# Row stages in chunks of 128 rows in place of 256, beside an LSTM that runs step by step

## What is computed

```
att = agg.reshape(n, 512) @ Wo.T + bo          # agg: attention sums, divided by their denominators
x2  = xn + att
z   = layernorm(x2) * g + b
h   = silu(z @ W1.T + b1)                      # 512 -> 1024
x   = x + x2 + h @ W2.T + b2                   # 1024 -> 512
y   = layernorm(x)
# LSTM over the rows as time, t = 0..1249, hidden size 512, four gates
gates_t = y_t @ Wx + b + h_{t-1} @ Wh
c_t = sigmoid(f) * c_{t-1} + sigmoid(i) * tanh(c~);  h_t = sigmoid(o) * tanh(c_t)
x   = x + h_t
```

## Time and profile before

| | us |
|---|---|
| median of 3 runs | 6714.76 |
| lowest, highest | 6714.20, 6720.42 |
| span of the profiled execution | 6560.1 |
| median of the runs less that span | 154.7 |
| PE busy | 5245.2 (80% of the span) |
| DVE busy | 3804.3 (58%) |
| ACT busy | 1879.1 (29%) |

### The profile page before, as it was taken

How to read it: one execution, slowest core, us unless ns; L and a number is a source line. 1 busy time by engine, 2 the same in 40 slices (tenths; PEclk the granted TensorE clock), 3 DMA queues, 4 the chain that set the end, 5 groups by cost and what they waited for, 6 DMA issues and landing times. The chain is left out here.

```text
span 6560.1 us, 407056 instructions
## 1 busy us (share of the span) xinstructions
PE 5245.2 (80%) x179105; PEld 3616.3 (55%) x179105; DVE 3804.3 (58%) x22336; ACT 1879.1 (29%) x8915; POOL 677.8 (10%) x716
## 2 busy tenths in 40 slices
PE   1989757789777888777887778987777777888999
PEld 1433334566555666556665556665555555554445
DVE  7337857466666666666666666666666666574111
ACT  1210069333333333333333333333333333200100
POOL 0744345000000000000000000000000000252000
PEclk8999979899999999999999999999999999998999
DMA  2235455101000000000000000100000000221110
GB/s 90 77 92 141 117 160 162 59 28 30 1 0 0 17 28 17 0 0 8 27 27 0 0 0 22 30 9 0 0 0 0 0 0 0 77 80 56 68 36 13
DMA packets 172012, 241.50 MB, mean 37 GB/s; under 512 B 90362, under 2 KB 130938, under 8 KB 167827
## 3 DMA queue, kind: packets, MB, share of 16 engines
q0 software_dynamic: 41952, 116.33, 6.5%
q1 hardware_dynamic: 129714, 120.73, 6.0%
HBM read 224.38 MB, written 12.61 MB: 36 GB/s over the span
## 5 line engine op out<-in xcount | busy, mean ns | idle before, releaser
L1654 PE MATMUL l_bank<-l_w,l_hp 128*32 128x128 f16 x160000 | 2486.7, 220 | 823.4 <-DVE l_hp L1942 801.0
L1654 PEld LDWEIGHTS l_bank<-l_w,l_hp 128*32 128x32 f16 x160000 | 2255.6, 97 | 1431.7 <-DVE l_hp L1942 1391.2
L1906 DVE STREAM_TRANSPOSE agg<-l_bank 128x128 f32<-128x128 f32 x2500 | 792.9, 317 | 1176.6 <-PE l_bank L1654 1005.9
L1782 ACT ACTIVATE l_th<-l_z 128x8 f32<-128x8 f32 x2500 | 523.7, 209 | 2153.2 <-DVE l_z L1912 2153.2
L1664 PE MATMUL l_spare<-l_w 128*2 128x512 f16 x12120 | 865.0, 379 | 3.7 <-issue 3.7
L2128 POOL DMA_INDIRECT ga_rows<-r_table,dst_t x176 | 166.9, 948 | 4633.8 <-DMA r_table<-c_r 4508.2
L1787 ACT ACTIVATE l_tc<-l_th 128x2 f32<-128x2 f32 x2500 | 490.5, 196 | 465.5 <-DVE l_th L1929 465.5
L1918 DVE SCALAR_TENSOR_TENSOR l_terms<-l_th 128x4 f32<-128x4 f32 x2500 | 357.0, 143 | 256.7 <-ACT l_th L1782 256.7
L1936 DVE TENSOR_TENSOR l_hp<-l_go,l_tc 128x2 f16<-128x2 f32 x2500 | 422.0, 169 | 132.0 <-ACT l_tc L1787 0.9
L1912 DVE TENSOR_REDUCE l_z<-agg 128x8 f32<-128x24 f32 x2500 | 447.5, 179 | 42.6
L1942 DVE TENSOR_TENSOR l_hp<-l_full,l_hp 128x2 f16<-128x2 f32 x2500 | 422.6, 169 | 43.9 <-DVE l_full L1937 0.6
(11 more groups left out here) (428 smaller groups left out, 4913.8 us busy)
## 6 DMA issues: line engine op xcount, KB each, us to landing
w<-in_g_W SPq DMA_DIRECT2D x128, 128.0 KB, 2.1
w<-in_l_Wx SPq DMA_DIRECT2D x128, 128.0 KB, 2.1
keys<-in_src_by_tile SPq DMA_DIRECT2D x7, 1344.0 KB, 6.8
e_w<-in_e_W SPq DMA_DIRECT2D x2, 4096.0 KB
e_chosen<-chosen SPq DMA_DIRECT2D x24, 256.0 KB, 6.2
wh<-in_l_Wh SPq DMA_DIRECT2D x1, 4096.0 KB, 18.8
late<-in_l_Wh SPq DMA_DIRECT2D x1, 4096.0 KB, 19.0
late<-in_l_Wx SPq DMA_DIRECT2D x1, 4096.0 KB
```

The source lines that it names most:

```text
L1654: mm = pe.matmul(banks[par][q][32 * j:32 * j + 32, 0:128], hp[:, par, k, 30 - 30 * v:62 - 30 * v], w16[:, half, k, j, 256 * q + 128 * v:25 ...
L1782: act.activation(th[:, 2 * q:2 * q + 2, 1:], z[:, q, :].rearrange("p (j m) -> p j m", m=GATES), ACT.Tanh, scale=2.0 ** -Z_BITS).then_inc(s ...
L1906: dve.transpose(turn[:, par, q, :, 1:33], banks[par][q][:, 0:128].rearrange("p (m r) -> p m r", r=32)).then_inc(s_turned[q], 1)
```

## The change

W becomes 128, so there are ten chunks: one before the recurrence and nine beside it, of 128 steps each, 102 of them with row work; steps 1152 to 1249 have none. A row operation has 128 columns in place of 256, and a turn one transpose in place of two.

The first chunk's Wx no longer goes into `late` behind the packing. Its first half goes into the room of W1 as soon as PE is done with FF1, its second half into the room of W2 as soon as PE is done with FF2. XIN waits for each half by itself. The pieces of chunk 1, which use the room of W1, wait for unit 7 of the first chunk's XIN.

With `late` no longer needed for Wx, packing is free to move: from steps 4 to 19 to six places in FF2 and ten in XIN. DVE's divisions of the later blocks (now nine, one stands ahead of the first turn) move from FF2 into XIN. The tile of the turned gates gets memory of its own, since the blocks are read until later.

```diff
-W = 256
-CHUNKS = RT * P // W
+W = 128
+PER = W // P
+CHUNKS = RT // PER
...
+PACK_AT = (*range(FF2, FF2 + 12, 2), *range(XIN, XIN + 30, 3))
+HALF_WX = KC * HID
...
-        turn = acc[:, 0:16 * 2 * SPREAD].rearrange("p (a q g e) -> p a q g e", a=2, q=2, g=GATES)
+        turn = sb("l_turn", [P, 16 * 2 * SPREAD]).rearrange("p (a q g e) -> p a q g e", a=2, q=2, g=GATES)
...
-        weights = {WO: wo_w2, FF1: w1[:, :, :].rearrange("p k n -> p (k n)"), FF2: wo_w2, XIN: late[:, :]}
+        w1_flat = w1[:, :, :].rearrange("p k n -> p (k n)")
+        def weights(stage, u, k):
+            at = (u * KC + k) * P
+            if stage == XIN:
+                room, at = (w1_flat, at) if at < HALF_WX else (wo_w2, at - HALF_WX)
+            else:
+                room = w1_flat if stage == FF1 else wo_w2
+            return room[:, at:at + P]
...
-            sp.wait_ge(s_packed, M16)
-            sp.dma_start(late[:, :], d["l_Wx"]).then_inc(wx_in, 16)
+            wait_pe(sp, 0, FF2 - 1)
+            sp.dma_start(w1_flat, d["l_Wx"][:, 0:HALF_WX]).then_inc(wx_in[0], 16)
+            wait_pe(sp, 0, LNL - 1)
+            sp.dma_start(wo_w2, d["l_Wx"][:, HALF_WX:]).then_inc(wx_in[1], 16)
             for c in range(1, CHUNKS):
-                used = [(c - 1, STEPS - 2 + p if c > 1 else FF2 - 1) for p in range(2)]
+                used = [(c - 1, STEPS - 2 + p if c > 1 else XIN + M16 - 1) for p in range(2)]
...
-                    if c == 0 and stage == XIN:
-                        pe.wait_ge(wx_in, 16)
+                    if c == 0 and stage == XIN and u % (M16 // 2) == 0:
+                        pe.wait_ge(wx_in[u // (M16 // 2)], 16)
...
-                for r in range(2):
-                    mm = pe.transpose(bank[:, r * P:(r + 1) * P], blocks[:, 2 * c + r, i * P:(i + 1) * P],
+                for r in range(PER):
+                    mm = pe.transpose(bank[:, r * P:(r + 1) * P], blocks[:, PER * c + r, i * P:(i + 1) * P],
                                       g.ident[:, :])
...
-                if WO <= i < WO + M16:
-                    v, o, s = packing(*divmod(i - WO, GATES))
-                    dve.wait_ge(s_high, i - WO + 1)
+                if i in PACK_AT:
+                    v, o, s = packing(*divmod(PACK_AT.index(i), GATES))
+                    dve.wait_ge(s_high, PACK_AT.index(i) + 1)
                     dve.scalar_tensor_tensor(o[:, 1], v, s, o[:, 0], ALU.mult, ALU.subtract).then_inc(s_packed, 1)
-                if FF2 + 4 <= i < FF2 + 4 + RT - 2:
-                    divide(i - FF2 - 2)
+                if XIN + 1 <= i < XIN + 1 + 3 * (RT - PER) and (i - XIN - 1) % 3 == 0:
+                    divide(PER + (i - XIN - 1) // 3)
```

More of the change, by code:

```diff
@@ L1498, in rows_and_lstm @@
         blocks = acc[:, :].rearrange("p (r w) -> p r w", r=RT)
-        turn = acc[:, 0:16 * 2 * SPREAD].rearrange("p (a q g e) -> p a q g e", a=2, q=2, g=GATES)
+        turn = sb("l_turn", [P, 16 * 2 * SPREAD]).rearrange("p (a q g e) -> p a q g e", a=2, q=2, g=GATES)
         denom = spare_column[:, 0:2 * RT * H].rearrange("p (a r h) -> p a r h", a=2, r=RT)
-        weights = {WO: wo_w2, FF1: w1[:, :, :].rearrange("p k n -> p (k n)"), FF2: wo_w2, XIN: late[:, :]}
-        piece = weights[FF1][:, 0:4 * P].rearrange("p (a k n) -> p a k n", a=2, k=2)
+        w1_flat = w1[:, :, :].rearrange("p k n -> p (k n)")
[6 more added lines that the diff above has]
+            return room[:, at:at + P]
+        piece = w1_flat[:, 0:4 * P].rearrange("p (a k n) -> p a k n", a=2, k=2)
         x2 = spare_rows[:, 0:KC * W].rearrange("p (k n) -> p k n", k=KC)
@@ L1525, in rows_and_lstm @@
         s_divided, s_high, s_packed, s_scaled, wx_in, w2_in = (sem("divided"), sem("high"), sem("packed"),
-                                                        sem("scaled"), sem("wx_in"), sem("w2_in"))
+                                                        sem("scaled"), pair("wx_in"), sem("w2_in"))
         piece_in = pair("piece_in")
@@ L1562, in _ @@
             sp.wait_ge(w2_in, 16)
-            sp.wait_ge(wx_in, 16)
             for p in range(2):
+                sp.wait_ge(wx_in[p], 16)
                 sp.wait_ge(piece_in[p], 16 * loads_of(CHUNKS, WO))
@@ L1595, in unit @@
                 for k in (2 * p, 2 * p + 1):
-                    w = piece[:, p, k % 2, :] if c > 0 else weights[stage][:, (u * KC + k) * P:(u * KC + k + 1) * P]
+                    w = piece[:, p, k % 2, :] if c > 0 else weights(stage, u, k)
                     mm = pe.matmul(bank[:, 0:W], w, src[:, k, :], start=k == 0, stop=k == KC - 1)
@@ L1635, in first_rows @@
             def first_rows():
-                pe.wait_ge(s_divided, 2)
+                pe.wait_ge(s_divided, PER)
                 for i in range(WO):
@@ L1706, in _ @@
                     step(t, t % 2)
-                pe.wait_ge(s_divided, 2 * c + 2)
+                pe.wait_ge(s_divided, PER * (c + 1))
                 wait_act(pe, c - 1, STEPS - 1)
@@ L1965, in _ @@
             g.link(dve, dve.reciprocal(denom[:, 0, :, :], denom[:, 0, :, :]))
-            divide(0)
-            divide(1)
+            for r in range(PER):
+                divide(r)
             g.link(dve, dve.memset(in_scale[:, 0, :], 2.0 ** (Z_BITS - 1)))
```

## The result

The change makes the kernel slower: 6757.27 us median of 4 runs (6747.47 to 6757.90) against 6717.24 us (6714.20 to 6720.42, 4 runs); ratio 1.0057, 95% interval 1.0045 to 1.0069. It is 40 us more, where 15 to 17 were forecast. The time lies in the range of 6706 to 6760 us, near its upper end, and outside the 6718 to 6748 us that belonged to the forecast itself.

What follows compares the result with a forecast made beforehand. It took the serial recurrence (3.413 us a step, row work almost wholly hidden) and the unhidden first chunk as the bound. 6560.1 - 41.4 + 59.2 = 6577.9, with 154.7 around it 6732.6, said as 6732 us; range 6706 to 6760.

Steps and rivals of the forecast that it cites:

- the forecast itself: Main case for the whole kernel: 6732 us, own range 6718 to 6748, chance 0.55.
- rival (b): Recurrence: one or two more gaps per chunk let PE's clock fall, 22 us more, 6754 us; chance 0.14.
- late instructions: Written-out recurrence steps: PE waits for instructions, 11.15 us a chunk, 100.4 us for nine chunks against 44.6.
- First chunk: Before the recurrence, all on the path: 41.4 us less of 103.9, bounds 34 and 50.
- turns and WO: First chunk's start, 11.9 us: one divide less ahead, shorter turns and four units; saves 6.0.
- XIN with the clearing: First chunk's last stretch: 31.8 us to 21.0 with packings moved in and DVE's clearing behind; saves 10.8.
- The loads: First chunk's W2 and l_Wx halves hide behind other stretches: cost nothing, up to 5 us if the cover went.
- Recurrence: Nine chunks in place of four: late instructions and FF2 stall sum to 118.4 against 59.2, 59.2 us more.
- the bound of 82: Recurrence's upper limit: 9 x 12.5 for late instructions plus 29 for stalls, less 59.2; lower limit 26.
- The stall: First FF2 unit of each chunk: PE waits for DVE's row operation, 2.0 us each, 18.0 against 14.6.
- The time outside the span: Whole kernel: 154.7 us between profile span 6560.1 and median 6714.76, left as it is and added to the total.
- The rule of the Trainium skill on hidden prefetch: Straight code's prefetch is hidden, branches stall; by it added chunks cost only their stall, 6677 us; counted under a 0.12 rival.

Runs made afterwards that it cites:

- e4: Changed kernel with chunks of 128, 256, 256, 256, 256 and 128 rows in place of ten of 128; 6541.94 us, ratio 0.9971 to the kernel before.
- e5: e4 with the wait at the first FF2 unit taken away; 6529.69 us, ratio 0.9956 to the kernel before.
- e6: e5 with DVE clearing the PSUM banks and small tiles ahead of the first chunk's XIN; 6529.11 us, ratio 0.9947 to the kernel before.
- e11: Changed kernel with one group of four filler matmuls in the steps that had none (turns, averages); 6606.58 us, ratio 1.0068 to the kernel before.
- e1: Kernel before, with 24 more recurrence steps without row work per chunk written out on PE in place of looped; 6782.87 us, ratio 1.0100 to it.
- e2: Changed kernel without the row work and weight piece loads of the nine chunks, steps still written out; 6727.26 us, ratio 1.0014 to the kernel before.
- e3: Changed kernel without the wait at the first FF2 unit; 6731.88 us, ratio 1.0021 to the kernel before.
- e7: Kernel before (chunks of 256) without the wait at the first FF2 unit; 6705.37 us, ratio 0.9986 to the kernel before.

## Why the prediction was right, and where it was short

The direction and the two mechanisms (a first chunk that shortens because nothing hides it, and a price for each chunk beside the recurrence) came out as forecast. The size did not: of 40 us more, 17 were forecast. The time is nearest to rival (b)'s 6754 us, but (b) had put 22 us to falls of the clock at gaps of late instructions, and the trace has 7.7 there.

- **First chunk: -41.4 forecast, -39.0 measured.** Stretch by stretch (forecast, then measured, from the earlier trace rows and those above): turns and WO 5.9 (11.9 less 6.0, 0.65 of it ahead of the stretch) and 8.4; first norm 9.2 and 9.3; FF1 10.8 and 10.3; FF2 7.9 and 7.4; second norm 7.7 and 7.9; XIN with the clearing 21.0 and 21.6. WO is what was off: it ran at PEclk 0.54, and its 32 matmuls took 6.6 us in place of 4.9 (5.2 to 5.6 in e4, e5 and e6). The loads cost nothing: no wait of PE there is on a DMA.
- **Recurrence: +59.2 forecast, +80.8 measured, just under the bound of 82.** The mechanism held and two terms were too small. Late instructions: 11.15 a chunk carried over from before, (140.4 - 23.9) / 9 = 12.9 measured, above the upper bound of 12.5 that the prediction gave the term, 16.1 us more in sum. 7.7 of it are five falls of the clock behind late instructions (5 x 1.54), of which the kernel before had none: rival (b)'s price, in part. Without them it is 12.1 a chunk. The stall: 2.0 a chunk, the middle between 1.5 without a fall of the clock and 2.6 with one, where the fall came 7 times of 9 and cost more than the 1.13 us taken from before (3.51 in place of 1.97 us): 23.9 in place of 18.0. The 1.13 was only a part of the price: in the earlier trace rows the slow stretch began in the unit, which took 1.59 us where four such matmuls take 1.13 at full pace, 0.46 more. The prediction counted the 0.46 to the wait and took them off again with the unit's width. In the changed kernel the unit keeps its 0.71 us, and the whole price, 1.54 us, falls on the small matmuls. Nor was PE idle for 2.24 us in all four stalls before (the earlier trace rows has 8.3 us for the four): the first was this one, with 1.55 us, and the clock fell there too:

```profile
1429.69 0.38 PE L1664 MATMUL l_spare<-l_w 128*2 128x512 f16 x1 [0.43 <-issue]
1431.62 1.14 PE L1597 MATMUL l_row_bank<-l_xp,w 128*128 128x256 f32 x4 [1.55 <-DVE l_xp L1877]
1432.68 3.53 PE L1654 MATMUL l_bank<-l_w,l_hp 128*32 128x128 f16 x128
```

Together the two terms are 22.0 us over; 21.6 were missing, and the steps behind the last chunk lost less than before.
- **The rest of that term**, 12.1 against 11.15, is open. It isn't the row work: without any, nine chunks lose 13.1 each, 11.4 with their ten falls taken out at the same 1.54 (two of them last 10.2 and 6.8 us in place of 3.4, so 11.4 is rather too much). It isn't missing work in the turns and averages (e11); for the unit steps that was not tried. Chunks of 256 rows differ by more within one kernel: 10.8 to 21.5 us in e6, 3.1 of the 21.5 for two falls; four were too few to read a mean from to better than a us or two. What makes one copy of the same code dearer than another, and so whether the clock falls behind its gaps, was not tried.
- **Total.** The time outside the span cancelled, but for a wrong reason: it was an earlier stage that runs 150 us longer in some sets of runs.
- The rule of the Trainium skill on hidden prefetch ("Runtime: NRT & Kernel Launch", Instruction fetch mechanics) is not borne out here: e1 shows 0.63 us lost per written-out step of some 280 PE instructions, while steps in a loop lose next to nothing (0.4 us in 98 of them). The prediction said that the looped steps contradict what the section of the Trainium skill says of branches, and that goes too far: it names a stall only for a target outside the blocks that the engine holds, and no run here shows where the target of these short loops lay. The same section of the Trainium skill says that a block is 16 KiB, 256 instructions; the packets agree, 105 of 16 KB for 96 steps of 280.

## What to carry to other kernels

Where work is hidden beside a serial chain, its size can be free, as here, while its number of pieces isn't: count what each piece adds to the chain, here written-out code and one wait, and split only the first piece, which nothing hides. On PE, a step written out once costs more than the same step in a loop where its instructions are short (some 280 in 3.4 us). The kernel with a short first chunk, long ones behind it, one semaphore more and two steps fewer written out beat both kernels: ratio 0.9918 (0.9905 to 0.9932) to the kernel before.

## What the runs showed that was not expected

- The kernel before takes 6716 us in one set of runs and 6560 in two others, each set within 21 us. Each of the three sets was on another chip; whether the chip makes the difference was not tried. The difference stands in the projections of the first layer (200 to 600 us), where engines wait for "remote", up to 21.8 us at a time; the five traces of the long kind (the changed kernel, e1, e2, e3 and e7) have these waits, and the eight of the short kind have none. What they wait for is open.
- The lower clock level can make the 128 small matmuls of a step take 3.51 us in place of 1.97, with PE idle for only 2.11 us ahead of them, and in one place of the changed kernel 3.56 us with an idle time of 1.36.
